# Start of a fused cross-attention and feed-forward kernel: warm-up operand, input queues, and the order of early VectorE and GpSimd work

## The chip, the cores and the metric

The kernel runs on one core of one Trainium2 chip. The time is the device time of one execution in microseconds (us), lower is better, and the figure compared is the median over runs.

## What is computed

The inputs are x (2 x 1024 x 256), a context of 2 x 77 x 256, four attention weights, two feed-forward weights, biases and two gates, all float32.

```python
def _layernorm(x): (x - mean) / sqrt(var + 1e-5)
def attn(x, context):                      # 8 heads of 64
    q = x @ Wq;  k = context @ Wk;  v = context @ Wv
    return softmax(q k^T / 8) v @ Wo + bo
def ffn(x):                                # fixed point, 8 bits
    h = relu(quant(quant(x) @ quant(w1).T + quant(b1)))
    return quant(h) @ quant(w2).T + quant(b2)
x = x + tanh(g_xattn) * attn(layernorm(x), ctx)
x = x + tanh(g_ffn) * ffn(layernorm(x))
```

## The kernel before

The 2048 rows of x are 16 tiles of 128 rows (T = 0 to 15; tiles 0 to 7 are batch 0, 8 to 15 batch 1). The weights of attention are folded first. `keysT` (L654) makes the transposed keys of both batches from the context and wk, `score_weights` (L662) multiplies them with the transposed wq, so that the scores of a tile are one product of the normalised rows with a 256 x 616 matrix `a_sb`; `output_weights` (L672) folds values and wo into `u_sb` in the same way. Both are kept as a high part (float32r) and a low part (what the rounding left), and a product is three passes: high by high, high by low, low by high.

Each engine's program is written out by hand as one list, and semaphores couple them. SyncE (L218) issues all input transfers, one after the other, on its own queue: context, wk, wq, tiles 0 and 1 of x, wv, tiles 2 and 3, wo, the two gates, b1, b2, then after a wait for constants of GpSimd bo, tiles 4 to 7, w1, tiles 8 to 15, w2. TensorE (L648) starts with `warm_up` (L650), five products of a constant tile `warm` that VectorE has set (L508), transposes the context (L810), does two more warm-up products, then the keys, the transposes of wq, the folded weights of batch 0, the value products and the first scores.

After that all engines run a loop over s = 0 to 15 (GpSimd to 19). In step s, TensorE transposes the normalised rows of tile s + 3 (L695), transposes the probabilities of tile s (`probsT`, L714, matmuls L722), does a share of the folded weights of batch 1 (s = 0 to 4), a half of the hidden layer, a tile of the output layer, the scores of tile s + 2 (L710) and the attention product of tile s (L741). `score_weights(1, 0)`, in step 0, waits for two low parts of `u_sb` (`u_ready` >= 2), because it writes into the banks h_ps from which VectorE takes them.

VectorE does the statistics of the first layer norm (`stats_first`, L517: bn_stats and bn_aggr of each tile), the maximum and the subtraction of it (`center`, L525), the sums of the softmax (`denominators`, L537), and the low parts (`u_low` L549, `rowsT_low` L553, `probsT_low` L560). Before the loop its order is center(0), stats_first(4, 8), denominators(0), u_low(0, 0), rowsT_low(2), center(1), u_low(0, 1), u_low(0, 2).

GpSimd turns the statistics into reciprocal deviations (`rstd_first`, L261: two small operations and a power, for a range of tiles at once), writes the normalised rows (`normalise_first`, L271), scales the probabilities (`softmax_scale`, L278), does the second layer norm (`normalise_second`, L283), some low parts (L298, L303), widens the hidden layer (L315) and adds a bias (L336). Where `rstd_first` stands is set by hand: ranges (0, 2), (2, 4), (4, 8) ahead of the loop, (8, 12) at the head of step 2, (12, 16) at the end of step 6. ScalarE copies PSUM to SBUF, and does exponentials and rounding; it issues no transfer.

```python
                pool.wait_ge(ve1_ready, 2 * len([T for T in FIRST_OF if T <= first]))
...
                if s == 0:
                    pe.wait_ge(u_ready, 2)
                    score_weights(1, 0)
```

Of the kernel before, what the change touches and what calls it, by code (L numbers as in the profile page):

```python
# [9 lines left out]
BF16 = mybir.dt.bfloat16  # L10
# [3 lines left out]
P = 128  # L14
# [3 lines left out]
INNER = H * HD  # L18
# [19 lines left out]
FIRST_OF = (0, 2, 4, 8, 12)  # L38
# [15 lines left out]
def flamingo_kernel(nc, x, ctx_in, g_xattn, g_ffn, wq, wk, wv, wo, bo, w1, b1, w2, b2, out):  # L54
    x_v = x.rearrange("b (p t) d -> p b t d", p=P)
    out_v = out.rearrange("b (p t) d -> p b t d", p=P)

    with ExitStack() as stack:
        def sb(name, shape, dt=F32):
            return stack.enter_context(nc.sbuf_tensor(name, shape, dt))  # L60
# [4 lines left out]
        def sem(name):  # L65
            return stack.enter_context(nc.semaphore(name))

        x_sb = sb("x_sb", [P, TILES, D])
# [15 lines left out]
        warm = sb("warm", [P, 512], BF16)  # L84
# [83 lines left out]
        def u_of(b, n, part):  # L168
# [8 lines left out]
        wk_in, wq_in, wv_in, wo_in, w1_in, w2_in = (sem(n) for n in ("wk_in", "wq_in", "wv_in", "wo_in", "w1_in", "w2_in"))  # L177
        g_in, bo_in, b1_in, b2_in = sem("g_in"), sem("bo_in"), sem("b1_in"), sem("b2_in")

        warm_set, zeroed, ident_set, consts, kz_zero, vz_zero, pad_set = (sem(n) for n in (  # L180
            "warm_set", "zeroed", "ident_set", "consts", "kz_zero", "vz_zero", "pad_set"))
# [37 lines left out]
        def _(sp):  # L219
            sp.dma_start(ctx_sb[:, :, :], ctx_in.rearrange("b m d -> m b d")).then_inc(ctx_in_sb, 16)  # L220
            sp.dma_start(wk_sb[:, :, :], wk.rearrange("(c p) n -> p c n", p=P)).then_inc(wk_in, 16)
# [4 lines left out]
            sp.dma_start(wo_sb[:, :, :], wo.rearrange("(c p) n -> p c n", p=P)).then_inc(wo_in, 16)  # L226
            sp.dma_start(g_sb[:, 0:1], g_xattn.rearrange("(a n) -> a n", a=1).to_broadcast([P, 1])).then_inc(g_in, 16)
# [4 lines left out]
            sp.wait_ge(consts, 3)  # L232
            sp.dma_start(bo_pad[0:1, :], bo.rearrange("(a n) -> a n", a=1)).then_inc(bo_in, 16)
            sp.dma_start(x_sb[:, 4:8, :], x_v[:, 0, 4:8, :]).then_inc(x_in[2], 16)
# [14 lines left out]
        def _(pool):  # L249
# [94 lines left out]
            rstd_first(4, 8)  # L344
            softmax_scale(0)

            for s in range(TILES + 4):
                if s == 2:
                    rstd_first(8, 12)
                if live(s + 4):  # L350
                    normalise_first(s + 4)
                if live(s - 1):
                    normalise_second(s - 1)
                if live(s + 1):
                    softmax_scale(s + 1)
                if s in (0, 1):
                    a_low(s, s + 1)
                if s == 3:
                    u_low(1)
                if s == 2:  # L360
                    hidden_bias()
                    output_bias()
                if 0 <= s - 4:
                    hidden_widen(s - 4)
                if s == 2:
                    add_bias(0)
                if live(s - 1) and s >= 2:
                    add_bias(s - 1)
                if s == 6:
                    rstd_first(12, 16)  # L370

        @block.scalar
        def _(act):
# [55 lines left out]

            act.wait_ge(ctxT_psum, 1)  # L430
# [76 lines left out]
        def _(dve):  # L507
            nc.vector.memset(warm[:, :], 1.0).then_inc(warm_set, 1)  # L508
# [94 lines left out]
            stats_first(4, 8)  # L603
            denominators(0)
            u_low(0, 0)
            rowsT_low(2)
            center(1)
            u_low(0, 1)
# [3 lines left out]
            for s in range(TILES):  # L612
# [15 lines left out]
                if s in (0, 1):  # L628
                    stats_first(8 + 2 * s, 10 + 2 * s)
                if s in (3, 5):  # L630
                    stats_first(9 + s, 11 + s)
# [17 lines left out]
        def _(pe):  # L649
            def warm_up(times):  # L650
                for _ in range(times):
                    nc.tensor.matmul(of_ps[:, 1, :], warm[:, 0:P], warm[:, :], start=True, stop=True)  # L652
# [151 lines left out]
            pe.wait_ge(warm_set, 1)  # L804
# [10 lines left out]
            pe.wait_ge(wk_in, 16)  # L815
            pe.wait_ge(ctxT_ready, 1)
            keysT(wk_sb, k_psum, (0, 1))
            keysT(wk_sb, k_psum, (2, 3))
# [101 lines left out]
```

## Time and profile before

| | |
|---|---|
| median of 3 runs | 131.03 us (130.72 to 131.44) |
| the profiled execution | 130.78 us |
| its span, first to last instruction | 129.0 us |
| TensorE matmul busy | 122.4 us, 95% |
| VectorE busy | 96.9 us, 75% |
| ScalarE busy | 73.7 us, 57% |
| GpSimd busy | 94.0 us, 73% |

The span lies within the profiled execution's time, with 1.8 us around it. PE is TensorE's matmuls, PEld its weight loads, DVE VectorE, ACT ScalarE, POOL GpSimd, SPq the sequencer of SyncE. A busy PE is not PE at its peak, since the ends of matmuls are modelled. L12 is line 12 of the kernel. A releaser in brackets is what ended the engine's idle time before the instruction.

### The profile page before, as it was taken

What the parts mean: (1) busy time and instruction counts of PE and PEld (TensorE: products, weight loads), DVE (VectorE), ACT (ScalarE), POOL (GpSimd) and SP (SyncE); (2) the same over time, 40 slices, a digit from 0 to 9 for tenths busy, and PEclk for the clock granted to TensorE, in tenths of its full rate; (3) what the DMA queues carried; (4) which work ended last, traced back from release to release, by engine and by line L of the source; (5) the groups of instructions that cost most, each with busy time, mean ns of one, the idle gap of its engine ahead of it and who ended that gap; (6) DMA issues with size and microseconds to landing.
All of it is one profiled execution on the core that took longest, in us unless ns stands there. A gap on an engine that the chain in (4) does not pass through costs nothing.

```text
span 129.0 us, 2744 instructions
## 1 busy us (share of the span) xinstructions
PE 122.4 (95%) x959; PEld 109.7 (85%) x959; DVE 96.9 (75%) x213; ACT 73.7 (57%) x155; POOL 94.0 (73%) x177
## 2 busy tenths in 40 slices
PE   5999999699999999999999999999999999999890
PEld 1789948599969799999999999999999998986680
DVE  5246797999987978999897978779797979543152
ACT  3154442697867778567292928374655729349620
POOL 4006609086989898998989898887959595997940
PEclk9999999999999999999999999999999999999999
DMA  3999994000000000000002000200010020020213
GB/s 79 334 300 319 407 408 198 4 3 0 5 0 0 3 0 8 0 0 0 5 0 81 0 0 5 81 3 0 35 51 0 0 81 0 8 81 0 81 36 132
DMA packets 5156, 8.86 MB, mean 69 GB/s; under 512 B 1148, under 2 KB 2199, under 8 KB 5015
## 3 DMA queue, kind: packets, MB, share of 16 engines
q1 hardware_dynamic: 5143, 8.69, 19.2%
q8 instruction: 8, 0.13, 0.4%
q14 instruction: 5, 0.04, 0.1%
HBM read 6.59 MB, written 2.10 MB: 67 GB/s over the span
## 4 chain that ended last, share of the span: by engine, by line
PE 89%; DVE 4%; POOL 3%; issue 1%; ACT 0%; DVEq 0%; POOLq 0%
PE of_ps L741 22%; PE sc_ps L710 21%; PE h_ps L765 9%; PE of_ps L774 7%; PE tr_ps L722 6%; PE h_ps L678 5%; PE tr_ps L658 4%; PE of_ps L652 2%; PE tr_ps L695 2%; PE h_ps L665 2%; POOL hid L315 2%; PE tr_ps L774 1%; PE sc_ps L774 1%; PE sc_ps L665 1%; PE of_ps L665 1%
## 5 line engine op out<-in xcount | busy, mean ns | idle before, releaser
L741 PE MATMUL of_ps<-u_sb,pT 128*128 128x256 f32 x240 | 31.2, 282 | 0.1
L710 PE MATMUL sc_ps<-a_sb,xT 128*128 128x308 f32 x192 | 31.2, 312 | 0.0
L741 PEld LDWEIGHTS of_ps<-u_sb,pT 128*128 128x128 f32 x240 | 29.9, 188 | 0.6 <-issue 0.6
L401 ACT ACTIVATE hid_q<-h_ps,b1z 128x256 int8<-128x256 f32 x62 | 26.4, 492 | 3.3 <-PE h_ps L765 3.3
L710 PEld LDWEIGHTS sc_ps<-a_sb,xT 128*128 128x128 f32 x192 | 27.6, 189 | 0.6 <-issue 0.4
L380 ACT ACTIVATE probs<-probs 128x616 f32<-128x616 f32 x16 | 11.6, 727 | 28.3 <-DVE probs L533 28.3
L280 POOL TENSOR_TENSOR probs<-probs,rden 128x616 f32<-128x616 f32 x16 | 19.6, 1228 | 3.4 <-DVE rden L543 3.4
L528 DVE TENSOR_REDUCE mx<-sc_ps 128x8 f32<-128x616 f32 x16 | 12.8, 798 | 9.1 <-PE sc_ps L710 9.1
L315 POOL CAST hid<-hid_q 128x512 bf16<-128x512 int8 x32 | 18.6, 612 | 0.9 <-ACT hid_q L401 0.9
L765 PE MATMUL h_ps<-x2T,w1T 128*128 128x256 bf16 x128 | 16.8, 273 | 0.1
L765 PEld LDWEIGHTS h_ps<-x2T,w1T 128*128 128x128 bf16 x128 | 12.3, 98 | 1.9 <-ACT hid_q L401 0.4
L392 ACT CAST pT<-tr_ps 128x640 fp32r<-128x640 f32 x16 | 11.1, 691 | 4.1 <-PE tr_ps L722 2.9
L533 DVE TENSOR_TENSOR probs<-sc_ps,mx 128x616 f32<-128x616 f32 x16 | 12.8, 802 | 0.6
L565 DVE TENSOR_TENSOR pT<-tr_ps,pT 128x640 fp32r<-128x640 f32 x16 | 12.6, 787 | 0.2 <-ACT pT L392 0.2
L774 PE MATMUL of_ps<-w2T,hid 128*128 128x256 bf16 x96 | 12.4, 273 | 0.0
L540 DVE TENSOR_REDUCE den<-probs 128x8 f32<-128x616 f32 x16 | 12.2, 763 | 0.0
L336 POOL TENSOR_TENSOR x_sb<-x_sb,b_gated 128x256 f32<-128x256 f32 x16 | 11.7, 733 | 0.1
L722 PE MATMUL tr_ps<-ident,probs 128*128 128x128 f32 x80 | 11.4, 273 | 0.0
L570 DVE SCALAR_TENSOR_TENSOR x_sb<-of_ps,tg,x_sb 128x256 f32<-128x256 f32 x16 | 7.7, 483 | 4.7 <-PE of_ps L741 3.3
L293 POOL TENSOR_SCALAR yq<-x_sb,nm,rstd 128x256 int8<-128x256 f32 x16 | 8.9, 555 | 1.8
L266 POOL TENSOR_SCALAR ve<-mv 128x4 f32<-128x4 f32 (+1 forms) x5 | 1.0, 196 | 12.1 <-DVE mv L523 12.0
L289 POOL TENSOR_TENSOR rstd<-ve,mhalf 128x1 f32<-128x1 f32 x16 | 8.8, 552 | 1.3
(107 smaller groups left out, 189.0 us busy)
## 6 DMA issues: line engine op xcount, KB each, us to landing
w_sb<-in_L_ffn_w_dram SPq DMA_DIRECT2D x2, 1024.0 KB, 11.0
out_dram<-x_sb SPq DMA_DIRECT2D x7, 256.0 KB, 2.5
x_sb<-in_x_dram SPq DMA_DIRECT2D x1, 1024.0 KB, 11.9
wk_sb<-in_L_xattn_Wk_dram SPq DMA_DIRECT2D x1, 512.0 KB, 3.7
wq_sb<-in_L_xattn_Wq_dram SPq DMA_DIRECT2D x1, 512.0 KB, 5.1
x_sb<-in_x_dram SPq DMA_DIRECT2D x2, 256.0 KB, 7.0
wv_sb<-in_L_xattn_Wv_dram SPq DMA_DIRECT2D x1, 512.0 KB, 7.4
wo_sb<-in_L_xattn_Wo_dram SPq DMA_DIRECT2D x1, 512.0 KB, 8.6
```

Source lines behind the costliest of these rows:

```text
L280: nc.gpsimd.tensor_tensor(probs_v(T), probs_v(T), rden[:, T % 2, :].unsqueeze(2).to_broadcast([P, H, M]), ALU.mult).then_inc(probs_ready, 1)
L315: nc.gpsimd.tensor_copy(hid[:, p, c:c + 2, :, :].rearrange("p c i r -> p (c i r)"), hid_q[:, (2 * k + n) % 4, :]).then_inc(hid_ready, 1)
L401: ins = nc.scalar.activation(hid_q[:, (2 * k + n) % 4, D * c:D * c + D], h_ps[:, n, D * c:D * c + D], ACT.Relu, bias=b1z[:, chunk:chunk + 1])
L528: nc.vector.tensor_reduce(mx[:, i, :].rearrange("p (a h) -> p a h", a=2), sc_v, AX.X, ALU.max).then_inc(max_ready, 1)
L533: nc.vector.tensor_tensor(probs_v(T).rearrange("p (a h) m -> p a h m", a=2), sc_v, mx[:, i, :].rearrange("p (a h) -> p a h", a=2).unsqueeze(3)
L540: nc.vector.tensor_reduce(den[:, i, :], probs_v(T), AX.X, ALU.add).then_inc(den_ready, 1)
L565: nc.vector.tensor_tensor(pT[:, T % 2, 1, :], pT_ps, pT[:, T % 2, 0, :].bitcast(F32), ALU.subtract).then_inc(pT_low, 1)
L710: ins = nc.tensor.matmul(sc_ps[:, a, 0:HALF], xT[:, T % 2, p, c, :], a_sb[:, q, T // TB, c, HALF * a:HALF * a + HALF], start=first, stop=last)
L722: ins = nc.tensor.transpose(pT_ps[:, P * c:P * c + P], probs[:, T % 2, P * c:P * c + P], ident[:, :])
L741: ins = nc.tensor.matmul(attn_ps, pT[:, T % 2, p, P * c:P * c + P], u_sb[:, q, MC * (T // TB) + c, :], start=first, stop=last)
L765: ins = nc.tensor.matmul(h_ps[:, n, D * c:D * c + D], w1T[:, d, P * chunk:P * chunk + P], x2T[:, p, d, :, :].rearrange("p i r -> p (i r)") ...
L774: ins = nc.tensor.matmul(ffn_of(T), hid[:, p, c, i, :], w2T[:, c, :], start=(c == 0), stop=(c == FC - 1))
```

## The change

The warm-up products read the framework's constant 1.0 in place of the tile `warm`, whose memset and semaphore go. wk comes in two transfers of 256 columns each, the first two instructions of ScalarE's program, with a semaphore each, and the keys of heads pairs 2 and 3 wait for the second. On SyncE's queue bo and tiles 4 to 7 stand ahead of the gates, b1 and b2. VectorE takes the early statistics two tiles at a time, at other steps, and u_low(0, 1) ahead of center(1). GpSimd's `rstd_first` has six calls instead of five: (4, 6) ahead of the loop, (6, 8) at the head of step 1, (8, 12) at the head of step 4.

```diff
--- before.py
+++ after.py
@@ -35,7 +35,7 @@
 AQ, WQ = 16.0, 64.0
 WARM = (5, 2)
 
-FIRST_OF = (0, 2, 4, 8, 12)
+FIRST_OF = (0, 2, 4, 6, 8, 12)
 
 
 
@@ -81,7 +81,6 @@
         ident = sb("ident", [P, P])
         ident_b = sb("ident_b", [P, P], BF16)
         bo_at = sb("bo_at", [P, P])
-        warm = sb("warm", [P, 512], BF16)
         mhalf = sb("mhalf", [P, 4])
 
         ctxT = sb("ctxT", [P, DK, MP])
@@ -174,11 +173,12 @@
-        wk_in, wq_in, wv_in, wo_in, w1_in, w2_in = (sem(n) for n in ("wk_in", "wq_in", "wv_in", "wo_in", "w1_in", "w2_in"))
+        wk_in = [sem(f"wk_in{j}") for j in range(2)]
...
@@ -218,20 +218,19 @@
         @block.sync
         def _(sp):
             sp.dma_start(ctx_sb[:, :, :], ctx_in.rearrange("b m d -> m b d")).then_inc(ctx_in_sb, 16)
-            sp.dma_start(wk_sb[:, :, :], wk.rearrange("(c p) n -> p c n", p=P)).then_inc(wk_in, 16)
             sp.dma_start(wq_sb[:, :, :], wq.rearrange("(c p) n -> p c n", p=P)).then_inc(wq_in, 16)
             sp.dma_start(x_sb[:, 0:2, :], x_v[:, 0, 0:2, :]).then_inc(x_in[0], 16)
             sp.dma_start(wv_sb[:, :, :], wv.rearrange("(c p) n -> p c n", p=P)).then_inc(wv_in, 16)
             sp.dma_start(x_sb[:, 2:4, :], x_v[:, 0, 2:4, :]).then_inc(x_in[1], 16)
             sp.dma_start(wo_sb[:, :, :], wo.rearrange("(c p) n -> p c n", p=P)).then_inc(wo_in, 16)
+            sp.wait_ge(consts, 3)
+            sp.dma_start(bo_pad[0:1, :], bo.rearrange("(a n) -> a n", a=1)).then_inc(bo_in, 16)
+            sp.dma_start(x_sb[:, 4:8, :], x_v[:, 0, 4:8, :]).then_inc(x_in[2], 16)
             sp.dma_start(g_sb[:, 0:1], g_xattn.rearrange("(a n) -> a n", a=1).to_broadcast([P, 1])).then_inc(g_in, 16)
             sp.dma_start(g_sb[:, 1:2], g_ffn.rearrange("(a n) -> a n", a=1).to_broadcast([P, 1])).then_inc(g_in, 16)
             sp.dma_start(b1_sb[:, :].rearrange("p (q e) -> p q e", e=2),
                          b1.rearrange("(q p e) -> p q e", p=P, e=2)).then_inc(b1_in, 16)
             sp.dma_start(b2_sb[:, :], b2.rearrange("(a n) -> a n", a=1).to_broadcast([P, D])).then_inc(b2_in, 16)
-            sp.wait_ge(consts, 3)
-            sp.dma_start(bo_pad[0:1, :], bo.rearrange("(a n) -> a n", a=1)).then_inc(bo_in, 16)
-            sp.dma_start(x_sb[:, 4:8, :], x_v[:, 0, 4:8, :]).then_inc(x_in[2], 16)
             sp.dma_start(w1_sb[:, :, :].rearrange("p (q e) d -> p q e d", e=2),
                          w1.rearrange("(q p e) d -> p q e d", p=P, e=2)).then_inc(w1_in, 16)
             sp.dma_start(x_sb[:, 8:16, :], x_v[:, 1, :, :]).then_inc(x_in[3], 16)
@@ -341,11 +340,13 @@
             rstd_first(2, 4)
             normalise_first(2)
             normalise_first(3)
-            rstd_first(4, 8)
+            rstd_first(4, 6)
             softmax_scale(0)
 
             for s in range(TILES + 4):
-                if s == 2:
+                if s == 1:
+                    rstd_first(6, 8)
+                if s == 4:
                     rstd_first(8, 12)
                 if live(s + 4):
                     normalise_first(s + 4)
@@ -427,6 +428,10 @@
                 for e in range(2):
                     nc.scalar.activation(dst[:, e, :, :], src[:, e, :, :], ACT.Copy, scale=1 / (WQ * AQ)).then_inc(w2T_ready, 1)
 
+            for j in range(2):
+                at = INNER // 2 * j
+                act.dma_start(wk_sb[:, :, at:at + INNER // 2],
+                              wk[:, at:at + INNER // 2].rearrange("(c p) n -> p c n", p=P)).then_inc(wk_in[j], 16)
             act.wait_ge(ctxT_psum, 1)
             nc.scalar.copy(ctxT[:, :, :].rearrange("p c n -> p (c n)"), sc_ps[:, 0, 0:DK * MP]).then_inc(ctxT_ready, 1)
             act.wait_ge(kz_zero, 1)
@@ -505,7 +510,6 @@
 
         @block.vector
         def _(dve):
-            nc.vector.memset(warm[:, :], 1.0).then_inc(warm_set, 1)
             nc.vector.memset(kz[:, :, :, :], 0.0).then_inc(kz_zero, 1)
             nc.vector.memset(vz[:, :, :, :], 0.0).then_inc(vz_zero, 1)
             for i in range(2):
@@ -600,12 +604,12 @@
             for q in range(2):
                 nc.vector.tensor_copy(head_blocks(vz, 1, q), pair_bank(1, q)).then_inc(v23_ready, 1)
             center(0)
-            stats_first(4, 8)
+            stats_first(4, 6)
             denominators(0)
             u_low(0, 0)
             rowsT_low(2)
+            u_low(0, 1)
             center(1)
-            u_low(0, 1)
             u_low(0, 2)
             dve.wait_ge(tg_ready, 1)
 
@@ -626,9 +630,9 @@
                 if live(s - 6):
                     result(s - 6)
                 if s in (0, 1):
-                    stats_first(8 + 2 * s, 10 + 2 * s)
-                if s in (3, 5):
-                    stats_first(9 + s, 11 + s)
+                    stats_first(6 + 2 * s, 8 + 2 * s)
+                if s in (3, 4, 5):
+                    stats_first(4 + 2 * s, 6 + 2 * s)
                 if live(s + 2):
                     center(s + 2)
             residual(TILES - 1)
@@ -649,7 +653,8 @@
         def _(pe):
             def warm_up(times):
                 for _ in range(times):
-                    nc.tensor.matmul(of_ps[:, 1, :], warm[:, 0:P], warm[:, :], start=True, stop=True)
+                    nc.tensor.matmul(of_ps[:, 1, :], nc.const_aps.tensor(1.0, [P, P], BF16),
+                                     nc.const_aps.tensor(1.0, [P, 512], BF16), start=True, stop=True)
 
             def keysT(w, done, pairs):
                 for j in pairs:
@@ -801,7 +806,6 @@
                                                   w2q[:, o, D * q:D * q + D].bitcast(BF16), ident_b[:, :])
                 ins.then_inc(wT_psum, 1)
 
-            pe.wait_ge(warm_set, 1)
             warm_up(WARM[0])
             pe.wait_ge(ident_set, 1)
             pe.wait_ge(ctx_in_sb, 16)
@@ -812,9 +816,10 @@
             ins.then_inc(ctxT_psum, 1)
             warm_up(WARM[1])
 
-            pe.wait_ge(wk_in, 16)
+            pe.wait_ge(wk_in[0], 16)
             pe.wait_ge(ctxT_ready, 1)
             keysT(wk_sb, k_psum, (0, 1))
+            pe.wait_ge(wk_in[1], 16)
             keysT(wk_sb, k_psum, (2, 3))
             pe.wait_ge(wq_in, 16)
             for j in range(PAIRS):
```

Three places where the order of instructions changes. The first is VectorE, from center(0) (L528, L533 before; L532, L537 in the changed file, whose lines are numbered anew) to the first low part of the probabilities. Before:

```order
L533 TENSOR_TENSOR probs<-sc_ps,mx 128x8x77
L520 BN_STATS st<-x_sb 128x6 x4
L523 BN_AGGR mv<-st 128x2 x4
L540 TENSOR_REDUCE den<-probs 128x8
L543 RECIPROCAL rden<-den 128x8
L551 TENSOR_TENSOR u_sb<-h_ps,u_sb 128x512
L556 TENSOR_TENSOR xT<-tr_ps,xT 128x256
L528 TENSOR_REDUCE mx<-sc_ps 128x8
L533 TENSOR_TENSOR probs<-sc_ps,mx 128x8x77
L551 TENSOR_TENSOR u_sb<-h_ps,u_sb 128x512
L551 TENSOR_TENSOR u_sb<-of_ps,u_sb 128x256
L565 TENSOR_TENSOR pT<-tr_ps,pT 128x640
```

and in the changed kernel:

```order
L537 TENSOR_TENSOR probs<-sc_ps,mx 128x8x77
L524 BN_STATS st<-x_sb 128x6 x2
L527 BN_AGGR mv<-st 128x2 x2
L544 TENSOR_REDUCE den<-probs 128x8
L547 RECIPROCAL rden<-den 128x8
L555 TENSOR_TENSOR u_sb<-h_ps,u_sb 128x512
L560 TENSOR_TENSOR xT<-tr_ps,xT 128x256
L555 TENSOR_TENSOR u_sb<-h_ps,u_sb 128x512
L532 TENSOR_REDUCE mx<-sc_ps 128x8
L537 TENSOR_TENSOR probs<-sc_ps,mx 128x8x77
L555 TENSOR_TENSOR u_sb<-of_ps,u_sb 128x256
L569 TENSOR_TENSOR pT<-tr_ps,pT 128x640
```

Two tiles of statistics instead of four stand there, and the second low part from h_ps now comes ahead of the maximum of tile 1.

The second is GpSimd from the scaling of tile 1's probabilities (step 0) into step 2. Before:

```order
L280 TENSOR_TENSOR probs<-probs,rden 128x8x77
L298 TENSOR_TENSOR a_sb<-full,a_sb 128x616
L275 TENSOR_SCALAR xn<-x_sb,nm,rstd 128x256
L286 TENSOR_SCALAR ve<-mv 128x1
L287 TENSOR_SCALAR nm<-mv 128x1
L289 TENSOR_TENSOR rstd<-ve,mhalf 128x1
L293 TENSOR_SCALAR yq<-x_sb,nm,rstd 128x256
L280 TENSOR_TENSOR probs<-probs,rden 128x8x77
L298 TENSOR_TENSOR a_sb<-full,a_sb 128x616
L266 TENSOR_SCALAR ve<-mv 128x4
L267 TENSOR_SCALAR nm<-mv 128x4
L269 TENSOR_TENSOR rstd<-ve,mhalf 128x4
```

and in the changed kernel:

```order
L279 TENSOR_TENSOR probs<-probs,rden 128x8x77
L297 TENSOR_TENSOR a_sb<-full,a_sb 128x616
L265 TENSOR_SCALAR ve<-mv 128x2
L266 TENSOR_SCALAR nm<-mv 128x2
L268 TENSOR_TENSOR rstd<-ve,mhalf 128x2
L274 TENSOR_SCALAR xn<-x_sb,nm,rstd 128x256
L285 TENSOR_SCALAR ve<-mv 128x1
L286 TENSOR_SCALAR nm<-mv 128x1
L288 TENSOR_TENSOR rstd<-ve,mhalf 128x1
L292 TENSOR_SCALAR yq<-x_sb,nm,rstd 128x256
L279 TENSOR_TENSOR probs<-probs,rden 128x8x77
L297 TENSOR_TENSOR a_sb<-full,a_sb 128x616
```

A trio for two tiles (128x2) has come in ahead of step 1's normalised rows, and the trio for four tiles (128x4) that followed step 1 has gone to step 4.

The third is the head of ScalarE's program, here in the changed kernel:

```order
L433 DMA wk_sb<-in_L_xattn_Wk_dram 128x2x256 x2
L436 ACT_TABLE_LOAD
L436 COPY ctxT<-sc_ps 128x308 [waits ctxT_psum]
L440 COPY kz<-tr_ps 64x2x2x77 [waits k_psum,kz_zero]
L440 COPY kz<-tr_ps 64x2x2x77
```

Before, the table load was its first instruction, and the one transfer of wk was SyncE's second.

## Rows read from the trace of the kernel before

**Rows 1.** The page: span, and busy time of each engine

```profile
span 129.0 us, 2744 instructions
...
PE 122.4 (95%) x959; PEld 109.7 (85%) x959; DVE 96.9 (75%) x213; ACT 73.7 (57%) x155; POOL 94.0 (73%) x177
```

**Rows 2.** The chain that ended last: start us, us, what

```profile
1.44 2.31 PE of_ps L652 x5
...
5.12 2.89 PE tr_ps L658 x16
...
11.49 1.05 PE tr_ps L658 x8
...
21.83 0.81 DVE mx L528
...
23.47 0.61 DVE u_sb L551
```

**Rows 3.** Timeline, 0 to 5 us: start, us, engine, line, operation, [idle before <-releaser]

```profile
0.30 0.10 POOL L907 MEMSET const-bfloat16-1.0<- 128x1 bf16 x1
...
0.72 1.28 ACT L431 ACT_TABLE_LOAD   x1 [0.72 <-PEq L907]
...
0.90 0.48 DVE L508 MEMSET warm<- 128x512 bf16 x1 [0.90 <-PEq L907]
...
3.36 0.68 PEld L810 LDWEIGHTS sc_ps<-ident,ctx_sb 77*128 77x128 f32 x4 [0.51 <-issue]
...
4.99 2.79 PEld L658 LDWEIGHTS tr_ps<-ctxT,wk_sb 128*128 128x128 f32 x16 [0.77 <-DMA wk_sb<-in_L_xattn_Wk_dram]
```

**Rows 4.** Windows: busy us (starts) per engine, granted clock, DMA share, GB/s

```profile
2.00:3.00 1.00, 1.00 (x4) 0.30 (x2) 0.78 (x2) 0.00 (x0) 0.29 (x2) 1.00 0.87 162
```

**Rows 5.** Timeline, 17 to 25 us, all engines

```profile
17.68 0.72 ACT L380 ACTIVATE probs<-probs 128x616 f32<-128x616 f32 x1 [2.80 <-DVE probs L533]
...
19.94 0.59 ACT L388 CAST u_sb<-h_ps 128x512 fp32r<-128x512 f32 x1 [0.66 <-PE h_ps L678]
...
21.83 0.80 DVE L528 TENSOR_REDUCE mx<-sc_ps 128x8 f32<-128x616 f32 x1 [0.80 <-PE sc_ps L710]
...
22.28 0.71 PE L722 MATMUL tr_ps<-ident,probs 128*128 128x128 f32 x5
...
23.62 0.38 ACT L376 CAST xT<-tr_ps 128x256 fp32r<-128x256 f32 x1
...
24.12 1.32 PE L665 MATMUL h_ps<-kz,wqT 128*128 128x154 f32 x8 [1.13 <-DVE u_sb L551]
24.31 0.81 DVE L565 TENSOR_TENSOR pT<-tr_ps,pT 128x640 fp32r<-128x640 f32 x1
```

**Rows 6.** Timeline of GpSimd, 26 to 31 us

```profile
26.15 1.23 POOL L280 TENSOR_TENSOR probs<-probs,rden 128x616 f32<-128x616 f32 x1 [3.44 <-DVE rden L543]
27.33 1.53 POOL L298 TENSOR_TENSOR a_sb<-full,a_sb 128x616 fp32r<-128x616 f32 x1
28.86 0.55 POOL L275 TENSOR_SCALAR xn<-x_sb,nm,rstd 128x256 f32<-128x256 f32 x1
30.22 0.19 POOL L286 TENSOR_SCALAR ve<-mv 128x1 f32<-128x1 f32 x1 [0.81 <-DVE mv L577]
```

**Rows 7.** Timeline of GpSimd, 12 to 15 us: a trio for two tiles, then normalised rows

```profile
12.94 0.19 POOL L266 TENSOR_SCALAR ve<-mv 128x2 f32<-128x2 f32 x1 [0.22 <-DVE mv L523]
...
14.38 1.09 POOL L275 TENSOR_SCALAR xn<-x_sb,nm,rstd 128x256 f32<-128x256 f32 x2
```

**Rows 8.** Windows of the loop, columns as in rows 4: PE, PEld, DVE, ACT, POOL

```profile
30.20:54.40 24.20, 24.20 (x190) 21.61 (x190) 20.99 (x46) 17.72 (x32) 22.22 (x39) 1.00 0.01 2
54.60:83.30 28.70, 28.70 (x243) 27.95 (x241) 24.61 (x51) 16.46 (x40) 26.57 (x48) 1.00 0.05 19
```

**Rows 9.** Timelines of GpSimd and TensorE, about 70 us: probabilities of tile 8

```profile
68.90 1.23 POOL L280 TENSOR_TENSOR probs<-probs,rden 128x616 f32<-128x616 f32 x1
...
70.74 0.71 PE L722 MATMUL tr_ps<-ident,probs 128*128 128x128 f32 x5
```

More of the change, by code:

```diff
@@ L176, in flamingo_kernel @@
         ctx_in_sb = sem("ctx_in_sb")
-        wk_in, wq_in, wv_in, wo_in, w1_in, w2_in = (sem(n) for n in ("wk_in", "wq_in", "wv_in", "wo_in", "w1_in", "w2_in"))
+        wk_in = [sem(f"wk_in{j}") for j in range(2)]
+        wq_in, wv_in, wo_in, w1_in, w2_in = (sem(n) for n in ("wq_in", "wv_in", "wo_in", "w1_in", "w2_in"))
         g_in, bo_in, b1_in, b2_in = sem("g_in"), sem("bo_in"), sem("b1_in"), sem("b2_in")
-        warm_set, zeroed, ident_set, consts, kz_zero, vz_zero, pad_set = (sem(n) for n in (
-            "warm_set", "zeroed", "ident_set", "consts", "kz_zero", "vz_zero", "pad_set"))
+        zeroed, ident_set, consts, kz_zero, vz_zero, pad_set = (sem(n) for n in (
+            "zeroed", "ident_set", "consts", "kz_zero", "vz_zero", "pad_set"))
         ctxT_psum, ctxT_ready = sem("ctxT_psum"), sem("ctxT_ready")
```

## The prediction

> **What bounds the kernel now.** I read the page first, then the chain that ended last, then timelines of the places that the change touches. TensorE's matmuls are busy for 122.4 of 129.0 us [rows 1], and the chain is almost nothing but PE: what shortens the kernel must take away TensorE work, a wait of TensorE, or its slow start. GpSimd's 73% on the page hides a second bound. Between 54.6 and 83.3 us it is busy for 26.57 of 28.70 us, and what is missing is short gaps between its operations; from 30.2 to 54.4 it is 22.22 of 24.20 [rows 8]. It works without a break there and is just ahead of TensorE. Its smallest margin is at tile 8: the scaling of the probabilities starts at 68.90 and ends at 70.13, and TensorE starts to transpose them at 70.74 [rows 9], 0.61 us later.
>
> Two things on the chain are not work. TensorE starts at 1.44, when VectorE's memset of `warm` (0.90 to 1.38) is over [rows 2, 3]. And it stands for 1.13 us before 24.12, where score_weights(1, 0) waits for the low part of `u_sb` that VectorE makes only after the 1.6 us of center(1) [rows 2, 5].
>
> **The clock at the start.** The granted clock reads 1.00 in the rows [rows 4], but the matmuls tell of two levels. Sixteen key matmuls at the start take 2.89 us on the chain and eight value matmuls of the same shape later 1.05 [rows 2], so sixteen would take 2.10; 0.79 is the cost of the slow level (1.2 GHz) over the first 1.6 us of the keys, so TensorE gets its 2.4 GHz at about 6.5 us. Each us by which this comes earlier saves half a us, and in the same way a us of delay ahead of it costs about half a us, since less work is left for the slow level.
>
> **Edit 1, warm-up from the constant.** The constant is there at 0.40 [rows 3]. The earliest of the other engines starts at 0.72 and VectorE at 0.90 [rows 3]; TensorE then starts between these, about 0.84, 0.6 earlier than 1.44. Its five products end near 3.1, and the context lets the weights be loaded only at 3.36 [rows 3], so no transposes come earlier. What may come earlier is the clock: by 0 to 0.6 us, which is worth 0 to 0.3. I take 0.3, as the activity begins 0.6 earlier and the pause after it is short. VectorE's next memsets start 0.5 earlier and nobody waits for them.
>
> **Edit 2, wk in two halves on ScalarE's queue.** The weight load of the first key matmul waited for wk and came at 4.99 [rows 3], while the warm-up products ended just before. With wk there in time that load goes beside them. It is worth 0 to 0.3 us, the length of such a load (0.17 on the average of rows 3, some more for the first); I take 0.2, which at the slow level is 0.1 on the end. The second half has eight matmuls of cover. ScalarE pays two issues ahead of a table load of 1.28 us and has nothing else to do until the context is copied, well after 3.36: hidden. Against this stands the context itself, which now shares the 16 DMA engines with wk from the start. It is 154 rows of 1 KB, and the engines moved 162 GB/s between 2 and 3 us [rows 4]: sharing evenly could cost it up to 154 KB / 162 GB/s = 0.95 us, and at least nothing, as its transfer is issued first. I take 0.2, so 0.1 on the end. (The Trainium skill, page "DMA: Bandwidth & Descriptors", section "Queues, rings and completion order", speaks against this edit: the queues of SyncE and ScalarE have rings on the same 16 engines, which alternate between them packet by packet, and a completion count lands only after all earlier writes of that engine, whichever queue they came from. By it the context would be late by most of what wk puts in between. No row before has two input queues, so none shows it.)
>
> The start is then worth 0.3 + 0.1 - 0.1 = 0.3 us, with ends of 0.3 + 0.15 = 0.45 gained and 0.95 / 2 = 0.5 lost.
>
> **Edit 3, the order of SyncE's queue.** Without wk each issue comes some 0.4 us earlier. bo and tiles 4 to 7 come earlier, the gates and biases behind half a MB more. The gates are needed for the tanh on ScalarE, behind which it idled 2.80 us before the first exponential at 17.68 [rows 5]; that idle time is the cover. Nothing is gained since no engine waited for any of these. Cost 0. Were the gates more than 2.8 us late, the first exponentials would be next.
>
> **Edit 4, VectorE.** Two tiles of statistics leave the stretch after center(0); they were hidden, and stay so. u_low(0, 1) costs 0.61 [rows 2] and needs ScalarE's copy, which ends at 19.94 + 0.59 = 20.53 [rows 5]. VectorE is idle for 0.80 before center(1) at 21.83 [rows 5], so the low part fits into that hole and center(1) doesn't move. The low part is ready at 21.2. TensorE is free for score_weights when its five transposes from 22.28 are done, at 22.99 [rows 5]: the wait of 1.13 us goes, all of it, and TensorE is 1.13 ahead. What is late next is not VectorE: the low part of tile 0's probabilities waits for a copy that ends at 23.62 + 0.38 = 24.00 [rows 5], and so starts at about 24.08 and not at 24.31. VectorE's later work, and with it the first release of GpSimd, comes 0.23 earlier, not 1.13.
>
> **Edit 5, GpSimd.** It scales tile 1 from 26.15 [rows 6], now from 25.92. It then makes a low part and, new in step 1, a trio for tiles 6 and 7. From its first operation to the normalised rows behind it such a trio takes 14.38 - 12.94 = 1.44 us [rows 7]. Before, GpSimd was idle here for 0.81 until 30.22, waiting for the first second-norm statistics [rows 6]; these now come 0.2 to 1.1 earlier, and of that idle time some 0.08 stays as the usual gap. The second norm of tile 0 so starts at 30.22 - 0.23 + 1.44 - 0.73 = 30.70, 0.48 **later** than before, though TensorE is 1.13 ahead. The trio for tiles 8 to 11 goes from step 2 to step 4: later in the order, the same work, nothing by step 5. Between 54.4 and 54.6 GpSimd was idle once more; of this I give back 0.17. So at tile 8 the scaling ends at 70.13 + 0.48 - 0.17 = 70.44 and TensorE can start its transposes at about 70.5, against 70.74: 0.27 us ahead is left of 1.13. The rest goes in several waits at `probsT`, of tiles 2, 5, 6 and 8. Beyond tile 8 the margin grows again (there is no trio after step 6), and the 0.27 stays to the end. That last term lies between 0 (the trio or the gaps come out 0.3 longer) and 1.13 (GpSimd catches up).
>
> **Sum.** The shift of 0.3 at the start moves all engines. 0.27 + 0.3 = 0.57 us. The profiled execution is at 130.78, which would go to 130.2; it stands 0.25 under the median of 131.03, which goes to about 130.4.
>
> **The rivals.**
> - *TensorE keeps all of the 1.13 us.* GpSimd makes up its 0.9 us, because VectorE and ScalarE, further ahead, let it start earlier than I reckon or its operations are shorter at other times. For: the trace shows no wait of TensorE on GpSimd in the loop. Against: rows 8, in which it has no idle time to draw on. 131.03 - 1.13 - 0.3 = 129.6.
> - *The start gives nothing.* The context comes up to 0.95 us late by sharing with wk and eats what the clock gives, 0.5 against 0.4; the trio takes what is left of the wait. 131.03 - 0.27 + 0.1 to 131.03: 130.9. This is where the rule on the two queues would lead. For: 16 engines moving 162 to 370 GB/s are shared by whatever is queued. Against: the context is issued first and is small.
> - *Slower: the pause keeps the clock low.* TensorE now runs dry from about 3.0 to 3.5, between the warm-up and the context. Before it worked without a pause from 1.44 and had the high level about 5 us later, at 6.5. If the rise came as late after the pause, at 3.5 + 5 = 8.5, the slow level would last 2.0 us longer and cost 1.0; with 0.27 + 0.1 gained the kernel would be 0.65 slower, 131.7. It decides if the rise comes later than about 7.3 us. Against: half a us of idleness after two of work is little.
> - That the change doesn't do what it says is excluded by the order of the instructions for VectorE and GpSimd; for the warm-up, that TensorE starts before 0.9 is open, and costs 0.05.
>
> **How the numbers follow.** A measurement of this kernel tells about 0.5% (0.65 us) from no change, that is a time under 130.4 or over 131.7. My forecast (0.55) lies at that edge, from 130.1 to 130.8; somewhat less than half of it, 0.25, counts as faster. The first rival has 0.2, all faster. The second has 0.17, all the same. The third has 0.08, of which 0.05 slower. Faster 0.45, same 0.50, slower 0.05. The range reaches from 129.5 to 131.1: it takes in the first and the second rival and leaves the third out.
>
> **What would show each step.** The first warm-up matmul near 0.84; the context's weight load at 3.4 to 3.6 and the keys' at 4.8 to 5.1; the sixteen key matmuls in about 2.5 us and not 2.89. No wait of TensorE before score_weights(1, 0), which starts about 1.4 earlier. GpSimd's first second norm without idle time before it, and only 0.2 us from where it was. Waits of TensorE's weight loads on GpSimd at L722, some 0.9 us in total, the last at tile 8. If TensorE waits for nobody there, the GpSimd step is wrong; if the keys take over 3 us, the clock step is; if the context's load comes after 3.9, sharing has cost more than I took.

## The result and the profile after

| | before | changed |
|---|---|---|
| median of 20 runs each, taken side by side | 130.76 us | 132.40 us |
| ratio, with 95% interval | 1 | 1.0112 (1.0091 to 1.0133) |
| profiled execution / its span | 130.78 / 129.0 us | 132.57 / 130.8 us |
| TensorE matmul busy in it | 122.4 us | 124.3 us |

The kernel is slower by 1.1%, about 1.5 us; the forecast was 0.6 us faster, with a range up to 131.1. Of the 20 runs of the changed kernel 18 lie at 131.87 to 134.27 and two at 130.74 and 131.41; of those of the kernel before 18 lie at 130.05 to 131.44 and two at 132.74 and 133.07. Every ratio here and below leaves out the runs over 1.5% above the fastest of the same kernel, and since these can be runs in which the clock rose late, the text gives them beside it.

The page of the changed kernel, beside [rows 1]:

```profile
span 130.8 us, 2748 instructions
...
PE 124.3 (95%) x959; PEld 110.8 (85%) x959; DVE 96.5 (74%) x212; ACT 73.4 (56%) x155; POOL 94.7 (72%) x180
```

TensorE has the same 959 matmuls and is busy for 1.9 us more. Where, the chain that ended last tells, in its first 10.5 us (start us, us, what), beside [rows 2]:

```profile
0.72 3.44 DMA ctx_sb<-in_ctx_dram
4.16 0.14 issue
4.29 0.75 PE sc_ps L814 x4
5.04 0.85 PE of_ps L656 x2
5.89 3.99 PE tr_ps L663 x16
9.88 0.45 PE h_ps L827 x4
```

The chain no longer starts with the warm-up but with the context's transfer, and the sixteen key matmuls take 3.99 us where they took 2.89. They end at 9.88, before at 8.01: 1.87 us later, which is the whole loss (the span grew by 1.8). The timeline of the same stretch shows the rest, beside [rows 3]:

```profile
0.72 0.97 ACTq L433 DMA_DIRECT2D wk_sb<-in_L_xattn_Wk_dram  x2
...
0.76 2.29 PE L656 MATMUL of_ps<-const-bfloat16-1.0 128*128 128x512 bf16 x5 [0.76 <-PEq L912]
...
4.26 0.55 PEld L814 LDWEIGHTS sc_ps<-ident,ctx_sb 77*128 77x128 f32 x4 [2.12 <-issue]
4.29 0.75 PE L814 MATMUL sc_ps<-ident,ctx_sb 77*128 77x77 f32 x4 [1.24 <-DMA ctx_sb<-in_ctx_dram]
```

TensorE starts at 0.76, 0.68 us earlier than before. The context's weights are loaded at 4.26 and not at 3.36: the context is 0.90 us late. Between, TensorE stands for 1.24 us. In the chain the keys start 0.77 later (5.89 against 5.12), which is the lateness less a little, since their first weight load no longer waits for wk; and they take 1.10 longer. That makes the 1.87.

The granted clock reads 1.00 in every row of the views, but the trace keeps the moment from which the full clock (2.4 GHz) was granted: 6.36 us in the kernel before, 9.55 in the changed one, measured from the first instruction. That fits the matmuls: all sixteen keys of the changed kernel run at the slow pace, and the transposes of wq behind them take the same 1.04 us in both.

In the middle, GpSimd's timeline beside [rows 6]:

```profile
29.04 1.53 POOL L297 TENSOR_TENSOR a_sb<-full,a_sb 128x616 fp32r<-128x616 f32 x1
30.66 0.19 POOL L265 TENSOR_SCALAR ve<-mv 128x2 f32<-128x2 f32 x1
...
31.98 0.56 POOL L274 TENSOR_SCALAR xn<-x_sb,nm,rstd 128x256 f32<-128x256 f32 x1
32.61 0.19 POOL L285 TENSOR_SCALAR ve<-mv 128x1 f32<-128x1 f32 x1
```

and the waits of TensorE's weight loads (us in total, times, longest), among them:

```profile
PEld tr_ps L727 <- POOL probs L279: 1.4, 4, 0.4
```

This is as forecast: a sixth trio, no idle time before the second norm, four waits at the transposes of the probabilities. The table below takes the start out. It counts from the first transpose of wq, right after the keys (7.85 us before, 9.72 in the changed kernel), to the starts of other matmuls, and to the last instruction.

| us after the first wq transpose | score_weights(1, 0) | probabilities, tile 6 | tile 7 | tile 8 | end |
|---|---|---|---|---|---|
| before | 16.27 | 50.78 | 56.83 | 62.90 | 121.15 |
| changed | 14.99 | 50.24 | 56.32 | 62.74 | 121.07 |
| e5, the orders alone | 15.00 | 50.34 | 56.44 | 62.87 | 121.28 |
| e6, u_low alone | 15.01 | 49.41 | 55.46 | 61.77 | 120.11 |
| e13, five trios | 14.99 | 49.39 | 56.80 | 62.90 | 121.19 |

Each row is one profiled execution. The changed kernel gains 1.28 us at score_weights, has 0.16 of it left at tile 8 and 0.08 at the end.

### The profile page after: what moved, and what is told of

Read it like the earlier page. It is cut to its first block, busy times and chain, and to the rows that moved or that the text cites. A ratio compares the mean times of both kernels' runs of the same rounds, so it can differ in the third digit from the quotient of the medians.

```text
span 130.8 us, 2748 instructions
## 1 busy us (share of the span) xinstructions
PE 124.3 (95%) x959; PEld 110.8 (85%) x959; DVE 96.5 (74%) x212; ACT 73.4 (56%) x155; POOL 94.7 (72%) x180
## 4 chain that ended last, share of the span: by engine, by line
PE 52%; POOL 33%; issue 5%; DVE 3%; DMA 3%; ACT 1%; POOLq 0%; DVEq 0%
PE of_ps L746 11%; PE sc_ps L715 11%; PE h_ps L770 6%; POOL probs L279 6%; PE of_ps L779 5%; PE tr_ps L663 5%; POOL hid L314 4%; PE tr_ps L727 4%; POOL x_sb L335 4%; POOL rstd L288 3%; POOL yq L292 3%; POOL xn L274 3%; DMA ctx_sb<-in_ctx_dram 3%; PE h_ps L683 2%; POOL a_sb L297 2%
## 5 line engine op out<-in xcount | busy, mean ns | idle before, releaser
L532 DVE TENSOR_REDUCE mx<-sc_ps 128x8 f32<-128x616 f32 x16 | 12.7, 791 | 8.8 <-PE sc_ps L715 8.8
L537 DVE TENSOR_TENSOR probs<-sc_ps,mx 128x616 f32<-128x616 f32 x16 | 12.8, 801 | 0.5
L265 POOL TENSOR_SCALAR ve<-mv 128x2 f32<-128x2 f32 (+1 forms) x6 | 1.2, 194 | 13.4 <-DVE mv L527 13.1
L727 PEld LDWEIGHTS tr_ps<-ident,probs 128*128 128x128 f32 x80 | 9.0, 141 | 1.4 <-POOL probs L279 1.4
## 6 DMA issues: line engine op xcount, KB each, us to landing
x_sb<-in_x_dram SPq DMA_DIRECT2D x1, 1024.0 KB, 10.5
```

The lines of the kernel that those rows point to most:

```text
L532: nc.vector.tensor_reduce(mx[:, i, :].rearrange("p (a h) -> p a h", a=2), sc_v, AX.X, ALU.max).then_inc(max_ready, 1)
L537: nc.vector.tensor_tensor(probs_v(T).rearrange("p (a h) m -> p a h m", a=2), sc_v, mx[:, i, :].rearrange("p (a h) -> p a h", a=2).unsqueeze(3)
L727: ins = nc.tensor.transpose(pT_ps[:, P * c:P * c + P], probs[:, T % 2, P * c:P * c + P], ident[:, :])
```

## The experiments

Each result is a ratio to the kernel before, timed side by side, with its 95% interval.

**e1, wk in one transfer on SyncE's queue again, all else changed.**

```diff
+            sp.dma_start(wk_sb[:, :, :], wk.rearrange("(c p) n -> p c n", p=P)).then_inc(wk_in, 16)
-                act.dma_start(wk_sb[:, :, at:at + INNER // 2], ...
```

> The changed kernel with wk in one transfer on SyncE's queue again, behind the context. Theory A (the context is late because wk is queued beside it on ScalarE's queue, and it is the pause of 1.24 us between the warm-up and the context that keeps TensorE slow until after the keys): the context's weight load is back at about 3.4 us, the pause is 0.3 to 0.5 us, the sixteen key matmuls take under 3 us, and the kernel is at 0.994 to 1.000 of the one before. Theory B (any pause after the warm-up does it, however short): the load is back at 3.4, but the keys still take about 4 us and the kernel is 1.004 to 1.010 of before.

1.0001 (0.9968 to 1.0033). Of 12 runs 8 lie at 129.87 to 131.17 and 4 at 131.81 to 131.97. In its profile, of a run of the first group (130.31):

```profile
3.23 0.74 PE L810 MATMUL sc_ps<-ident,ctx_sb 77*128 77x77 f32 x4 [0.18 <-DMA ctx_sb<-in_ctx_dram]
...
5.07 2.37 PE L659 MATMUL tr_ps<-ctxT,wk_sb 128*128 128x154 f32 x16 [0.25 <-DMA wk_sb<-in_L_xattn_Wk_dram]
```

Without the second queue the context is in time and the 1.1% are gone. The keys took 2.37 here, 0.5 less than before. In this run the high level came at 4.68, the earliest of all profiles, in spite of the pauses of 0.18 before the context and 0.25 before the keys. So B is refuted, and A holds for the profiled run. That the four runs near 131.9 had a late clock is likely by their times, and not seen.

**e2, changed kernel with 8 first warm-up products.**

```diff
-WARM = (5, 2)
+WARM = (8, 2)
```

> The changed kernel with 8 first warm-up products instead of 5, which end at about 4.2 us, just before the late context. Nothing is taken from the lateness. Theories A and B both say that the high clock comes during the keys or before, at 5.5 to 6.5 us, since TensorE no longer pauses; the keys end at about 8.5 us (before 8.0, changed 9.9), where the second half of wk, landing at about 7.6, may hold them. Ratio to before 1.000 to 1.004. Theory C (the clock has nothing to do with the pause; the slow keys come from reading wk while the transfers write, or from the constant as an operand): the keys take about 4 us as in the changed kernel, ratio 1.010.

1.0096 (1.0060 to 1.0132), more than expected.

```profile
5.51 1.65 PE L663 MATMUL tr_ps<-ctxT,wk_sb 128*128 128x154 f32 x8
8.04 1.09 PEld L663 LDWEIGHTS tr_ps<-ctxT,wk_sb 128*128 128x128 f32 x8 [1.12 <-DMA wk_sb<-in_L_xattn_Wk_dram]
8.04 1.32 PE L663 MATMUL tr_ps<-ctxT,wk_sb 128*128 128x154 f32 x8 [0.89 <-DMA wk_sb<-in_L_xattn_Wk_dram]
```

The pause is gone and so are the slow keys: eight take 1.65 and the other eight 1.32, and the high level comes at 6.30, though the context is late. C falls. But the time goes to two other waits: the context is still late (weight load at 4.08), and the second half of wk isn't there for another 0.89 us. In the changed kernel the slow keys had hidden that.

**e3, the warm-up from the constant alone, on the kernel before.** The edit is that of the change.

> The kernel before with the warm-up from the constant alone. First matmul at about 0.76, the context's load at 3.4, a pause of 0.3 us. Theory A: the high clock comes up to 0.6 us earlier, ratio 0.996 to 1.000. Theory B: the pause sets it back, the keys take about 4 us, ratio 1.006 to 1.010.

0.9995 (0.9955 to 1.0035), and that number hides what happens: of the 12 runs 6 lie at 130.07 to 131.03 and 6 at 131.82 to 132.50. The median of all is 131.43, against 130.85 for the kernel before, of whose 23 runs 22 lie at 130.01 to 131.37 and one at 132.75. The profile is of a run with the late clock (131.84): the chain has

```profile
5.03 4.04 PE tr_ps L657 x16
```

after a wait of 0.4 us for the context. Half of the runs gain a little, half lose about 1 us or more. The high level came at 8.61 in the profiled run; the other runs are put in the two groups by their times alone.

**e4, wk in two halves on ScalarE's queue alone.** The warm-up is the old one, from 1.44 us.

> The kernel before with wk in two halves on ScalarE's queue alone; the warm-up starts after VectorE's memset. The context is late by 0.9 us (load at 4.26) if two queues side by side cause it, or not late (3.4) if it was chance. The pause is then 4.26 less 3.6, some 0.6 us. Theory A: clock late by at most the shift, keys end some 0.5 us later, ratio 1.002 to 1.006. Theory B: keys at about 4 us, ratio 1.010 to 1.016.

1.0107 (1.0065 to 1.0149), as much as the whole change. Lateness is confirmed, the price is above A's and at the foot of B's.

```profile
4.13 0.75 PE L814 MATMUL sc_ps<-ident,ctx_sb 77*128 77x77 f32 x4 [0.37 <-DMA ctx_sb<-in_ctx_dram]
...
5.52 3.27 PE L662 MATMUL tr_ps<-ctxT,wk_sb 128*128 128x154 f32 x16
```

The context's load is 0.73 later than before, behind a pause of 0.37, and the keys take 3.27 (3.02 in the same view of the kernel before). The high level came at 7.28. This profile is one of the two fastest of its six runs (131.57 to 132.79); the keys of the slower ones were not seen.

**e9, wk as one transfer on ScalarE's queue, on the kernel before.**

```diff
+            act.dma_start(wk_sb[:, :, :], wk.rearrange("(c p) n -> p c n", p=P)).then_inc(wk_in, 16)
```

> The kernel before with wk as one transfer of 2 KB rows on ScalarE's queue, so that the halves are undone and only the second queue is left. If the second queue makes the context late, its weight load is at 4.1 to 4.3 as with the halves, ratio 1.004 to 1.012. If it was the halves with their 1 KB rows, the load is at 3.4 to 3.6 and the ratio 1.000 to 1.003.

1.0103 (1.0061 to 1.0145), 4 runs. The context's load is at 3.73, late by 0.37 in place of 0.7 to 0.9, which neither expectation had. So the second queue delays it, and by these single profiles the halves about double the delay; the time is lost with either. The profile is of the fastest run (131.58): it has no pause before the context, the high level at 7.49, and the first wq transpose 0.60 later than before.

**e10, a pause without lateness:** the constant, 3 products instead of 5, on the kernel before.

```diff
-WARM = (5, 2)
+WARM = (3, 2)
```

> The kernel before with the warm-up from the constant and 3 first products instead of 5: they end at about 2.2 us, the context comes at 3.4, so TensorE pauses for 1.2 us, as long as in the changed kernel, without any lateness of the context. If the pause makes the clock late: keys at about 4 us, most runs 1.0 to 1.7 us over the kernel before, ratio 1.007 to 1.013. If the late context or the second queue did: ratio 0.998 to 1.002.

1.0071 (1.0037 to 1.0104). None of the 11 runs lies among the 130s: five are at 131.19 to 131.48 and six at 131.93 to 133.27. The profile is of the second group (132.17).

```profile
3.44 0.75 PE L808 MATMUL sc_ps<-ident,ctx_sb 77*128 77x77 f32 x4 [1.24 <-DMA ctx_sb<-in_ctx_dram]
...
4.83 4.45 PE L657 MATMUL tr_ps<-ctxT,wk_sb 128*128 128x154 f32 x16
```

With the context in time and one input queue, a pause of 1.24 us goes with the changed kernel's slow keys, and the high level came at 9.16. Neither lateness nor a second queue is needed for it. The edit also takes two products away, so it doesn't part the pause from the smaller amount of warm-up work; the changed kernel, e1 and e3 do, since all three have five products from 0.76 and differ in the pause.

**e8, the constant with 6 products, on the kernel before,** so that TensorE works until the context is there.

> The kernel before with the warm-up from the constant and 6 products instead of 5, which end at about 3.4, so that TensorE doesn't pause before the context. Theory A/B together (it is the pause that makes the clock late in some runs): no run with the keys slow to the end, all runs within 1.3 us of each other as before, ratio 0.996 to 0.999. Rival (an earlier start is worth nothing or makes the rise more scattered): spread of over 2 us as with 5 products, ratio 1.000 or more.

0.9980 (0.9958 to 1.0001). 11 of 12 runs lie at 130.28 to 130.97, one at 132.79. The group of six at 132 is gone. An earlier start is then worth about 0.3 us by the medians (130.59 against 130.87), which the interval doesn't tell from nothing. The same start in e11 and e14 below leaves more late runs.

**e11, the changed kernel with both mended** (wk on SyncE, 6 products).

> The changed kernel with wk in one transfer on SyncE's queue and 6 first warm-up products: no late context, no pause; the orders of SyncE, VectorE and GpSimd are the changed ones. If the late context and the pause are all that made it slower, no run has the late clock, and the ratio is that of the two harmless parts together, 0.996 to 0.999.

1.0019 (0.9984 to 1.0054): no measurable difference; 8 of 10 runs lie at 130.46 to 130.95, two at 132.36 and 132.50. The expected small gain was not seen.

**e5, the orders of VectorE and GpSimd alone.**

> The kernel before with the reordering of VectorE and GpSimd alone (both parts, six calls of rstd_first). Theory G (GpSimd without idle time decides: the sixth trio eats what TensorE gains): score_weights(1, 0) starts 1.1 us earlier after the keys than before, TensorE then waits at the transposes of the probabilities of tiles 2, 5, 6 and 8, and the end is 0 to 0.27 us earlier: ratio 0.998 to 1.000. Rival H (the wait of 1.13 us is worth its length, and what the changed kernel lost lies in its start alone): ratio 0.990 to 0.993.

0.9989 (0.9964 to 1.0014). One of 12 runs is at 133.10. G holds: row e5 of the table is 1.27 ahead at score_weights, 0.03 at tile 8 and nothing at the end, with four waits at the probabilities:

```profile
PEld tr_ps L724 <- POOL probs L280: 1.5, 4, 0.5
```

**e6, one move alone.**

```diff
-            center(1)
             u_low(0, 1)
+            center(1)
             u_low(0, 2)
```

> The kernel before with one move alone: u_low(0, 1) ahead of center(1), statistics and rstd_first as before. Theory G: GpSimd has no sixth trio and draws on 0.81 us less nothing; it starts 0.23 earlier and the margin of 0.61 at tile 8 is used up: 0.7 to 1.0 us earlier, ratio 0.992 to 0.995. A rival, that VectorE's hole of 0.80 is too small with four tiles of statistics ahead of it and center(1) is late: 0.2 to 0.4 us less. A second rival, that the order on VectorE is worth nothing without the smaller first batch of statistics: ratio 1.000.

0.9927 (0.9898 to 0.9956): 0.7% faster, from two lines; 9 of 10 runs lie at 129.19 to 130.41, one at 131.79. VectorE's hole was large enough, with four tiles of statistics ahead of it:

```profile
20.84 0.68 DVE L551 TENSOR_TENSOR u_sb<-h_ps,u_sb 128x512 fp32r<-128x512 f32 x1
...
21.72 0.80 DVE L528 TENSOR_REDUCE mx<-sc_ps 128x8 f32<-128x616 f32 x1 [0.20 <-PE sc_ps L710]
```

center(1) still waits 0.20 for TensorE. GpSimd is the next bound here too, but at tile 8 alone:

```profile
PEld tr_ps L722 <- POOL probs L280: 0.3, 1, 0.3
```

**e13, the changed orders with five trios.** VectorE's batches of two stay; ranges (4, 6), (6, 10), (10, 16).

```diff
-                if s == 1:
-                    rstd_first(6, 8)
-                if s == 4:
-                    rstd_first(8, 12)
+                if s == 2:
+                    rstd_first(6, 10)
+                if s == 6:
+                    rstd_first(10, 16)
```

> VectorE's order and two-tile statistics as in the changed kernel, GpSimd with five trios instead of six: (4, 6) ahead of the loop, (6, 10) at the head of step 2, (10, 16) at the head of step 6; the start as before. Theory G (the sixth trio on GpSimd is what eats the gain): TensorE loses nothing at tiles 2, 5 and 6 and the end is 0.7 to 1.0 us earlier, ratio 0.992 to 0.995. Rival (the smaller batches of statistics on VectorE, which stand ahead of center in more steps, are what eats it): ratio 0.998 to 1.000, as with both parts.

1.0002 (0.9974 to 1.0031), which by its number speaks for the rival. Ten of 12 runs lie at 130.46 to 131.31 and two at 132.92 and 132.93, although the start is that of the kernel before. The trace doesn't. Up to tile 6 it is level with e6 (49.39 and 49.41 in the table) and 0.95 ahead of e5: VectorE's batches cost nothing, the sixth trio did. Then my own edit gave it all back in one place. The trio for six tiles stands at the head of step 6, ahead of tile 7's probabilities, where before a trio stood behind them:

```profile
58.86 0.21 POOL L266 TENSOR_SCALAR ve<-mv 128x6 f32<-128x6 f32 x1
...
59.51 1.34 POOL L269 TENSOR_TENSOR rstd<-ve,mhalf 128x6 f32<-128x6 f32 x1
...
63.32 1.22 POOL L280 TENSOR_TENSOR probs<-probs,rden 128x616 f32<-128x616 f32 x1
```

and TensorE waits for it once, in its waits:

```profile
PE tr_ps L722 <- POOL probs L280: 1.2, 1, 1.2
```

**e14, the same with the constant and 6 products.**

> The same with the warm-up from the constant and 6 products. If the two parts add, 0.2 to 0.3 us under the same without it, ratio 0.989 to 0.993; if the start gives nothing, 0.992 to 0.995.

1.0006 (0.9983 to 1.0029). Of 13 runs 9 lie at 130.33 to 131.07 and 4 at 132.51 to 133.01. It was expected to be faster, but has the order of e13 with its wait of over 1 us in the loop. Its profile is of the second group and has the keys slow throughout, with the high level at 9.65:

```profile
3.34 0.74 PE L808 MATMUL sc_ps<-ident,ctx_sb 77*128 77x77 f32 x4
3.88 1.06 PE L650 MATMUL of_ps<-const-bfloat16-1.0 128*128 128x512 bf16 x2
5.40 4.43 PE L657 MATMUL tr_ps<-ctxT,wk_sb 128*128 128x154 f32 x16 [0.46 <-DMA wk_sb<-in_L_xattn_Wk_dram]
```

There is no pause before the context, but one of 0.46 before the keys, for a late wk. One profile can't show that this pause was the reason: e1 and e7 have one of 0.25 and 0.23 at the same place and the keys fast.

**e7, the two good parts together:** e6 with the constant and 6 products.

> u_low(0, 1) ahead of center(1), and the warm-up from the constant with 6 products; inputs, statistics and rstd_first as before. If both theories hold, the gains add: 0.7 to 1.0 from the order and 0 to 0.3 from the start, ratio 0.990 to 0.994. If only the one on the order does, 0.992 to 0.995.

0.9907 (0.9872 to 0.9942), 6 runs at 129.09 to 130.01: the best ratio here, 129.72 against 130.87 in the median, though its interval overlaps that of e6, whose median is 129.68. So the orders' gain is there, and a gain of the start on top of it isn't shown. In its profile the keys are done 0.28 earlier than in e6 (first wq transpose at 7.43, there 7.71), and VectorE then waits for tiles 0 and 1 of x:

```profile
9.26 0.75 DVE L518 BATCH_NORM_STATS2 st<-x_sb 128x6 f32<-128x256 f32 x2 [0.57 <-DMA x_sb<-in_x_dram]
```

**e12, the same with wk in two halves, both on SyncE's queue.**

> u_low(0, 1) ahead of center(1), the constant with 6 products, and wk in two halves, both on SyncE's queue behind the context: the keys' first weight load no longer waits for all of wk. Gain against the same without the halves 0 to 0.15 us (the load beside the warm-up) or a loss of 0 to 0.2 us (one more issue ahead of wq and all that follows, 1 KB rows); ratio 0.989 to 0.993.

1.0019 (0.9991 to 1.0047), 12 runs at 130.00 to 131.57: the halves take the whole gain back. In the profile, of a run at 131.27, the keys start earlier, at 4.79, but wq, and tiles 0 and 1 of x, come later, and TensorE waits for wq:

```profile
8.43 1.10 PE L825 MATMUL h_ps<-ident,wq_sb 128*128 128x128 f32 x8 [0.89 <-DMA wq_sb<-in_L_xattn_Wq_dram]
```

## Why the prediction was wrong

**Edits 1 and 2, the start: wrong, and this is the step that failed.** I had +0.3 us gained with an end of 0.5 lost; the trace has 1.87 lost. Two terms failed and then acted on each other.

- *The context's lateness* was put at 0.2 within 0 to 0.95; it was 0.90 in the profile and 0.73 in e4, near the upper bound worked out from 162 GB/s [rows 4]. (The rule taken from the Trainium skill, "DMA: Bandwidth & Descriptors", "Queues, rings and completion order", agrees with the trace: the context's load went from 3.36 to 4.26 when wk was queued beside it. It deserved more than the 0.17 it had as a rival.) That the context is issued first and is small was no argument: its issue began at 0.72, and so did that of wk.
- *The clock* was taken to rise up to 0.6 us earlier, because the activity begins earlier. The products start 0.68 earlier, but with a pause of 1.24 us behind them the high level came at 9.55, not 6.36, after nearly all of the keys: sixteen took 3.99 and they would take 2.10 at the high level. e10, with the same pause and a context in time, has the high level at 9.16 and no run among the 130s; e2, with a late context and no pause, has it at 6.30. With a pause of 0.2 to 0.4 us and the same five products, half of the runs of e3 and a third of those of e1 are late by their times. Six products leave one late run of 12 in e8, none of 6 in e7, but two of 10 in e11 and four of 13 in e14.
- *That a delay ahead of the rise costs half of its length* was the wrong rule to join the two. It supposes a rise at a fixed time. Here the earlier start and the delay together made the pause, and with the pause the rise came later, so the keys started later and were slow as well: 0.77 + 1.10.

The third rival had the right mechanism, with a chance of 0.08, and about half the size: a rise at 8.5 against 9.55, and a kernel 0.65 us slower against about 1.5. It was priced with a context in time, the second with a clock in time. What happened is both together, a case that I hadn't written down.

**The second half of wk** was said to have "eight matmuls of cover". That held only as long as these were slow; in e2 they were not, and it cost 0.89.

**Edit 3, SyncE's order: at nothing, not tested alone.** e11, which holds it, shows no difference beyond its interval.

**Edit 4, VectorE: right.** The hole of 0.80 took the low part, center(1) did not move, the wait of 1.13 us went (score_weights starts 1.28 earlier in the table).

**Edit 5, GpSimd: right, a little small.** I forecast the second norm of tile 0 to start 0.48 later; counted from the first wq transpose it is 32.61 - 9.72 = 22.89 against 30.22 - 7.85 = 22.37, 0.52 later. At tile 8 I forecast 0.27 left; it was 0.16, and 0.08 at the end. The four waits are at the forecast tiles, 2, 5, 6 and 8, and sum to 1.4 us where I had some 0.9. The first rival, all 1.13 kept, is refuted by e5. That the sixth trio is the reason is shown by e13 up to tile 6, and by e6, which has no sixth trio and keeps 1.04 to the end.

**Open.** What sets the moment of the rise. In one profile each, the eight kernels without a pause before the context or the keys (before, e2, e5, e6, e8, e11, e12, e13) have it at 5.68 to 6.36; with short pauses it came at 4.68 (e1), 5.18 (e7), 7.28 (e4), 8.61 (e3) and 9.65 (e14); in e9, without a pause that the view shows, at 7.49; with 1.24 us at 9.16 and 9.55. So the long pause goes with a late rise each time and a short one doesn't decide it. Of the 121 runs of the kernel before in all comparisons 8 are over 132.5 us, with neither pause nor second queue; no profile is of such a run. That e9 loses 1.0% is not explained by its profile, which is of its fastest run and 0.6 us longer than the kernel before.

## What to carry to other kernels

Let a TensorE warm-up reach without a gap to the first real work: its length is set by when the first input lands and not by how early it can start. Moving the start alone opened a gap here, and cost more in half of the runs than it gave in the others. What a gap of a few tenths of a us costs is open; one of 1.24 us cost most. Before a transfer is put on a second queue, ask which small transfer at the head of the first one everything waits for: here it landed 0.4 to 0.9 us later. And where a wait is removed, list what the next engine in line has to do per step: here two lines of order were worth 0.7%, and a seemingly free split of a small operation (three instructions, 1.3 us on an engine almost without idle time) gave it all back.

## What the runs showed of the hardware that was not expected

- A start of the warm-up 0.68 us earlier, with a pause of 1.24 us behind it, went with the 2.4 GHz level 3.2 us later (9.55 against 6.36): on the chain sixteen 154-column matmuls took 3.99 us where 2.89 were seen before, and 4.25 in e10 with the same pause. The granted clock reads 1.00 in the views throughout; the level shows in the durations of equal matmuls and in the moment of the rise that the trace keeps.
- The rise came at 4.68 to 9.65 us over the kept traces of kernels that all start their warm-up at 0.76 or 1.44, and pauses of 0.2 to 0.5 us went with both ends of that range.
- The earlier start with a pause of 0.38 us split the times of one kernel in two groups about 1 us or more apart (e3: 6 of 12 runs at 130.1 to 131.0, 6 at 131.8 to 132.5), which a median over few runs does not show.
- wk on a second queue delayed a 154 KB transfer that was issued at the same time by 0.37 us in one piece of 2 KB rows (e9, one profile) and by 0.7 to 0.9 us in two of 1 KB rows (three profiles).
